# Zero rows at fixed places in the front, x1 split chunk by chunk, and group tables made inside the shared block

## What is computed

```python
xw = gelu(layernorm(ada_emb) @ w1 + b1) @ w2 + b2      # -> x_a, x_b: (b, 512, 8)
layer = base + einsum('bdr,bkr->bdk', x_a, x_b)
x1 = x + (x + einsum('btc,bco->bto', x, layer))

shared = (silu(x1 @ w1) * (x1 @ w3)) @ w2
s = sigmoid(concat([x1, t_emb]) @ router_W)
idx = top_k(s + router_bias, 2)                        # two experts per token
gates = s[idx] / sum(s[idx])
routed = sum over the two experts of gate * (gelu(x1 @ W1e[e]) @ W2e[e])
out = x1 + (shared + routed) / 3
```

## Time and profile before

| what | value |
|---|---|
| median of 3 runs | 1117.33 us (1116.65 to 1117.41) |
| the profiled execution, its own time | 1117.86 us |
| its span in the trace | 1116.1 us |
| TensorE busy with matmuls | 1076.1 us (96% of the span) |
| VectorE, ScalarE, GpSimd busy | 485.5, 398.7, 155.7 us |
| granted TensorE clock, mean | 0.986 of full speed |
| zero rows `xs_d<-zeros` | 8 DMAs of 1024 KB |

### The profile page before, as it was taken

One profiled execution on the slowest core, in us unless ns is written; L12 is line 12 of the kernel. 1 busy time (PEld: TensorE's weight loads), 2 busy tenths in 40 slices (PEclk: granted clock), 3 DMA queues, 4 the chain that ended last, 5 costly groups with the idle time before them and its releaser, 6 DMA issues.

```text
span 1116.1 us, 15418 instructions
## 1 busy us (share of the span) xinstructions
PE 1076.1 (96%) x5226; PEld 879.0 (79%) x5226; DVE 485.5 (44%) x1014; ACT 398.7 (36%) x687; POOL 155.7 (14%) x193
## 2 busy tenths in 40 slices
PE   6999799889799999999999999999999999999998
PEld 5666578778588888888888888888888888888886
DVE  4102654554356645655664533331424333142434
ACT  2211344441366566656666631211212121121211
POOL 3001258370000000000000022011020201102020
PEclk8999899999899999999999999999999999999999
DMA  8663579889768688767657545013050501305041
GB/s 302 267 229 98 186 274 395 300 287 307 208 189 278 191 239 272 223 193 213 212 150 194 183 132 207 1 58 132 0 188 0 187 0 55 133 0 188 0 151 38
DMA packets 131703, 191.42 MB, mean 172 GB/s; under 512 B 9535, under 2 KB 73023, under 8 KB 129879
## 3 DMA queue, kind: packets, MB, share of 16 engines
q1 hardware_dynamic: 120118, 156.38, 43.8%
q0 software_dynamic: 11552, 34.61, 8.3%
HBM read 117.04 MB, written 73.92 MB: 171 GB/s over the span
## 4 chain that ended last, share of the span: by engine, by line
PE 85%; DVE 5%; DMA 3%; SPq 3%; issue 2%; POOL 1%; ACT 1%; DVEq 0%; ACTq 0%; POOLq 0%
PE K L1461 10%; PE K L1462 10%; PE K L1463 10%; PE L L1462 5%; PE L L1463 5%; PE L L1461 5%; PE Rb L1462 5%; PE Rb L1463 5%; PE Rb L1461 5%; PE M L1461 4%; PE M L1463 4%; PE M L1462 4%; PE Rb L1551 3%; PE M L1489 2%; PE M L1491 2%; PE M L1490 2%
## 5 line engine op out<-in xcount | busy, mean ns | idle before, releaser
L462 ACT ACTIVATE slf<-K 128x512 f32<-128x512 f32 x64 | 38.3, 598 | 226.4 <-PE K L1463 221.9
L773 POOL DMA_INDIRECT yb<-ys_d,pos_fix x64 | 61.2, 957 | 322.4 <-DVE total L1392 254.0
L465 ACT CAST gTh<-slf 128x512 fp32r<-128x512 f32 x64 | 39.7, 621 | 184.9 <-DVE slf L475 184.9
L1461 PE MATMUL M<-w2h,gTh 128*128 128x512 f32 x256 | 100.5, 392 | 3.3 <-DVE gTl L477 3.3
L1463 PE MATMUL M<-w2h,gTl 128*128 128x512 f32 x256 | 100.3, 392 | 0.0
L1462 PE MATMUL M<-w2l,gTh 128*128 128x512 f32 x256 | 100.2, 391 | 0.0
L1461 PE MATMUL K<-x1h,w13h 128*128 128x512 f32 x256 | 99.7, 389 | 0.0
L1463 PE MATMUL K<-x1h,w13l 128*128 128x512 f32 x256 | 99.6, 389 | 0.0
L1462 PE MATMUL K<-x1l,w13h 128*128 128x512 f32 x256 | 99.6, 389 | 0.0
L475 DVE TENSOR_TENSOR slf<-L,slf 128x512 f32<-128x512 f32 x32 | 22.1, 692 | 161.8 <-PE L L1463 152.9
L1329 DVE TENSOR_TENSOR e2l<-e2raw,e2h 128x512 fp32r<-128x512 f32 x64 | 41.3, 686 | 79.9 <-ACT e2h L926 79.9
(11 more groups left out here) (244 smaller groups left out, 2470.2 us busy)
## 6 DMA issues: line engine op xcount, KB each, us to landing
w2c<-in_L_cond_w_dram SPq DMA_DIRECT2D x8, 2048.0 KB, 8.6
e1raw<-in_L_cond_W1e_dram SPq DMA_DIRECT2D x16, 1024.0 KB, 7.1
e2raw<-in_L_cond_W2e_dram SPq DMA_DIRECT2D x16, 1024.0 KB, 5.6
xr<-xs_d SPq DMA_DIRECT2D x64, 256.0 KB, 4.4
ys_d<-yo SPq DMA_DIRECT2D x32, 512.0 KB, 7.1
xtok<-in_x_dram SPq DMA_DIRECT2D x32, 256.0 KB, 7.5
x_d<-x1tok SPq DMA_DIRECT2D x8, 1024.0 KB, 8.4
xs_d<-zeros SPq DMA_DIRECT2D x8, 1024.0 KB, 8.8
```

Source lines behind the costliest of these rows:

```text
L462: nc.scalar.activation(slf[:, h % 2], U[h % 2][:], ACT.Silu).then_inc(ffn.silu, 1)
L465: nc.scalar.copy(gTh[:, h % 2], slf[:, h % 2]).then_inc(ffn.g_hi, 1)
L773: pool.indirect_dma_start(out=yb[:, c, :], out_offset=None, in_=ys_d, in_offset=bass.IndirectOffsetOnAxis(ap=pos_fix[:, c:c + 1].bitcast(U ...
L1461: mm(o, ah, bh_, start=start, stop=False)
```

## The change

- The zero rows no longer depend on the counts. SyncE writes the first 512 rows of each of the 8 regions with zeros, in the front: two behind the load of block 2's tokens, six behind the load of block 3's. They come from a zero tile `padz` (128 x 2048) that GpSimd fills at the start and that lies on the memory of `x1tok0`. So ScalarE's first copy into `x1tok0` and GpSimd's first scatter wait for `pad_out`.
- An expert's last group now ends with the expert's last token: where its last group would run past it, the group starts earlier and overlaps the group before. `tables` has more steps for that, and `rows_at_ends` moves the affected rows of `ypos`.
- x1 of block 7 is split chunk by chunk (`cut_last`) inside block 7, behind each `keep_base`, instead of all four chunks behind the block.
- `tables` moves from ahead of the shared block to behind its step 0, together with the cut of piece UP_PIECES + 1. `rows_at_ends` stands behind step 4, `gate_weights` behind step 5.
- SyncE's stream behind block 7: the table's store and load come between the last two `w2` pieces, the zero rows are gone, and `load_rows(0)` comes ahead of `load_e1(0)` and `load_e2(0)`.

```diff
@@ memory
+            with ExitStack() as z:
+                padz = sb("padz", [P, GR // P, D], F32, z)
             x1tok0 = sb("x1tok0", [P, TT, D], F32, st)
...
@@ SyncE, front
             for t in range(TT):
                 load_x(2, t)
+
+            def fill_pads(e):
+                sp.wait_ge(padz_rdy, 1)
+                sp.dma_start(xs_d[e * REGION:e * REGION + GR, :].rearrange("(p r) d -> p r d", p=P), padz[:]
+                             ).then_inc(pad_out, 16)
+            for e in range(2):
+                fill_pads(e)
             for n in range(5, LOADS):
                 load_net(n)
             for t in range(TT):
                 load_x(3, t)
+            for e in range(2, E):
+                fill_pads(e)
...
@@ SyncE, behind block 7
-            for i in range(UP_PIECES + 1, PIECES):
-                load_piece(sp, i)
+            load_piece(sp, UP_PIECES + 1)
             store_tok(NB - 1)
-
+            load_piece(sp, UP_PIECES + 2)
             sp.wait_ge(tabs, 1)
             sp.dma_start(tab_d, tabi[0:TAB]).then_inc(tab_out, 16)
-
-            pad_src = zeros[:].unsqueeze(1).broadcast_to([P, GR * D // (P * P), P])
-
-            def fill_pads(e):
-                alone(sp)
-                row = sp.value_load(padi[0:1, ds(e, 1)], min_val=0, max_val=E * REGION - GR)
-                sp.dma_start(xs_d[ds(row, GR), :].rearrange("(p r) (k c) -> p (r k) c", p=P, c=P), pad_src).then_inc(pad_out, 16)
-            sp.wait_ge(pads, 1)
-            with sp.Fori(0, E // 2) as e:
-                fill_pads(e)
             sp.wait_ge(tab_out, 16)
             sp.dma_start(tab_i[:], tab_d.rearrange("(a p) c -> a (p c)", a=1)).then_inc(tab_in, 16)
-            with sp.Fori(E // 2, E) as e:
-                fill_pads(e)
+            load_piece(sp, UP_PIECES + 3)
...
+            load_rows(0)
             load_e1(0)
             load_e2(0)
-            sp.wait_ge(pad_out, 16 * E)
-            load_rows(0)
...
@@ GpSimd
+            nc.gpsimd.memset(padz[:], 0.0).then_inc(padz_rdy, 1)
             pool.wait_ge(consts, 14)
...
+            pool.wait_ge(pad_out, 16 * E)
             for b in range(NB):
...
@@ ScalarE, keep_tok
                 if t == 0:
-                    if b == 1:
+                    if b == 0:
+                        act.wait_ge(pad_out, 16 * E)
+                    elif b == 1:
...
+            def cut_last(k):
+                act.wait_ge(xp_sb, (NB - 1) * KC + k + 1)
+                act.wait_ge(s_ps, NB)
+                nc.scalar.copy(x1h[:, k], xp[(NB - 1) % EARLY][:, k]).then_inc(x1_hi, 1)
...
                     if h % 2 == 1:
                         keep_base(b, h // 2)
+                        if b == NB - 1:
+                            cut_last(h // 2)
...
-            for k in range(KC):
-                act.wait_ge(xp_sb, (NB - 1) * KC + k + 1)
-                nc.scalar.copy(x1h[:, k], xp[(NB - 1) % EARLY][:, k]).then_inc(x1_hi, 1)
...
@@ tables
-            link(ts(col[ROW], tmp[0], float(E * REGION - GR), None, ALU.min))
+
+            link(ts(top, taken[:], -float(GR), None, ALU.add))
+            link(nc.vector.scalar_tensor_tensor(out=top, in0=iota8[:], scalar=float(REGION), in1=top,
+                                                op0=ALU.mult, op1=ALU.max))
+            link(tt(thr[:, 0:E - 1], top[:, 1:E], top[:, 0:E - 1], ALU.subtract))
+            link(tt(thr[:, 0:E - 1], thr[:, 0:E - 1], past[:, 0:E - 1], ALU.mult))
+            link(red(tmp[1], thr[:, 0:E - 1], AX, ALU.add))
+            link(tt(tmp[1], tmp[1], top[:, 0:1], ALU.add))
+            link(tt(col[ROW], tmp[0], tmp[1], ALU.min))
             link(ts(col[LAST], ends[:, E - 1:E], -1.0, None, ALU.add))
             nc.vector.tensor_copy(tabi[:], tab[:]).then_inc(tabs, 1)
 
-            nc.vector.tensor_scalar(t9, nt, float(GR), -float(REGION), ALU.mult, ALU.add).then_inc(tabs, 1)
+
+            link(ts(off, nt, float(GR), -float(GR), ALU.mult, ALU.add))
+            link(nc.vector.scalar_tensor_tensor(out=thr, in0=iota8[:], scalar=float(REGION), in1=off,
+                                                op0=ALU.mult, op1=ALU.add))
+            link(tt(off, thr, top, ALU.subtract))
+            link(ts(off, off, 0.0, None, ALU.max))
+            link(ts(t9, nt, float(GR), -float(REGION), ALU.mult, ALU.add))
+            tt(t9, t9, off, ALU.subtract).then_inc(tabs, 1)
...
+        def rows_at_ends(dve):
...
+            thr, off = tw[:, 6], tw[:, 7]
+            for e in range(E):
+                link(nc.vector.tensor_scalar(step[:], pos_all[:], thr[:, e:e + 1], off[:, e:e + 1], ALU.is_ge, ALU.mult))
+                link(nc.vector.tensor_tensor(slots[:], slots[:], step[:], ALU.add))
             nc.vector.tensor_copy(ypos[:], slots[:]).then_inc(tabs, 1)
...
@@ VectorE
+            def cut_last(k):
+                dve.wait_ge(x1_hi, k + 1)
+                if k == KC - 2:
+                    corrected(dve, NB - 2)
+                if k == KC - 1:
+                    corrected(dve, NB - 1)
+                tt(x1l[:, k], xp[(NB - 1) % EARLY][:, k], x1h[:, k].bitcast(F32), ALU.subtract).then_inc(x1_lo, 1)
...
+                    if b == NB - 1 and h % 2 == 1:
+                        cut_last(h // 2)
             places(NG - 1)
-            nc.vector.tensor_copy(padi[:], taken[:]).then_inc(pads, 1)
             cut_piece(UP_PIECES)
-            tables(dve)
...
-            after = {h: lambda h=h: cut_piece(UP_PIECES + 1 + h) for h in range(PIECES - UP_PIECES - 1)}
+            def tables_and_cut():
+                tables(dve)
+                cut_piece(UP_PIECES + 1)
+            after = {0: tables_and_cut, 1: lambda: cut_piece(UP_PIECES + 2), 2: lambda: cut_piece(UP_PIECES + 3)}
             after[3] = lambda: rows_in_ys(dve)
-            after[4] = lambda: gate_weights(dve)
+            after[4] = lambda: rows_at_ends(dve)
+            after[5] = lambda: gate_weights(dve)
```

15 lines of the change are left out of this document (9 added, 6 removed).

## The result

| kernel | median of its runs | against the kernel before |
|---|---|---|
| before, beside it | 1116.99 us (1116.65 to 1117.41) | |
| after | 1134.93 us (1130.55 to 1135.64) | 1.015 [1.0128, 1.0171] |

The kernel is 18 us slower; 1112.6 us had been predicted. The profiled execution took 1135.24 us (span 1133.3), 17.4 more than that of before. The losses lie in three stretches, and the gain that was predicted is there as well.

A forecast was written before the change was run, and what follows sets the result against it. TensorE, saturated in the last 800 us, was taken as the bound, so only earlier stretches could gain. 4.78 + 0.3 - 0.3 = 4.8 us off gave 1112.6 us, with 1109.7 to 1115.9 for 8 in 10.

The forecast's parts named there:

- The gap, 4.78 us: TensorE's 8.19 us idle ahead of the first expert group falls to 3.4 us, gaining 4.78 us.
- The clock, 0.3 us: At the first expert group, a shorter gap lets TensorE's clock fall less: 0.3 us gained, bounds 0 to 2.1.
- Three edits and what they move: The prediction's frame: price the change's edits and what they shift; the last 800 us were taken as saturated loops.
- The memset, "nothing": At the start, GpSimd's 1.8 us memset of the zero tile fits inside 7.56 us of its waiting: no cost.
- The zero rows in the front, 0.3 us: Six zero DMAs behind block 3's tokens slow small transfers ahead of the low-rank matmuls: 0.3 us lost, bounds 0 to 3.
- rival 2: The zero rows in the front slow the factors: 2 to 3 us lost, 1115 us; chance 0.12.
- The 2.77 us stall: TensorE's idle time at 240.15 in the shared block, tied to block 5's scatter, stays about 2.8 us.
- x1 split 0: Splitting x1 inside block 7 gives or costs nothing, as the scatter stall absorbs small shifts; without cover about 0.6 us.
- token store 0: Block 7's 1 MB token store, issued at about 233 beside the scatter, costs 0, bounds 2.5 us both ways.
- Table 0: Tables behind step 0 of the shared block leave step 1's low part half a microsecond early: 0 us lost.
- The signs named ahead of the result: Wrong if the first low-rank matmul or shared block starts over 1 us later, or TensorE waits again between 244 and 290.
- Rival 4: ScalarE's first copy into x1tok0 waits for slow zero DMAs and stops the chain of blocks: 1136 us; chance 0.06.

The follow-up runs named there:

- e16: e7 with the split of x1 and the move of the tables also undone; 1110.52 us beside 1116.67 for the kernel before, ratio 0.9957.
- e4: e1 with GpSimd's memset of padz moved behind its b2rep copies; 1119.61 us, 1.0027 of the kernel before.
- e1: The kernel after with 32 bytes per partition put back in padi's place; 1123.68 us, 1.0065 of the kernel before.
- e5: e4 without GpSimd's wait for the zero rows ahead of its first scatter; 1143.59 us beside 1138.57 for the kernel before, ratio 1.0037.
- e7: e5 with the eight zero DMAs also spread in pairs over idle DMA stretches; 1140.13 us beside 1138.57 for the kernel before, ratio 1.0005.
- e14: The same kernel as e5, run again; 1.0025 of the kernel before, which took 1139.20 us beside it.
- e13: The same kernel as e7, run again; 0.9998 of the kernel before, which took 1139.20 us beside it.
- e9: e4 with GpSimd's wait for the zero rows replaced by one for the long-ready constants; 1140.26 us beside 1139.47 for the kernel before, ratio 1.0.
- e2: The kernel before with 32 bytes per partition added behind tab, shifting x1h and all tiles behind; 1130.62 us, 1.0121 of the kernel before.
- e3: e1 with another 32 bytes ahead of all tiles, so weights and inputs both lie at 32 modulo 64; 1121.52 us, 1.0049 of the kernel before.
- e12: e7 with the group tables made ahead of the shared block as before; 0.9982 of the kernel before, which took 1139.47 us beside it.
- e15: The same kernel as e12, run again; 0.9964 of the kernel before, which took 1139.20 us beside it.
- e18: The same kernel as e12, run a third time; 0.9972 of the kernel before, which took 1134.87 us beside it.

## Why the prediction was wrong

- **The gap, 4.78 us: right.** Predicted was an idle time of 3.3 to 3.6 us, ended by the rows' low part, with the turns directly behind the expert weight's low part; it is 3.01 in the kernel after and 3.17 in e16. I had the first matmul of the group at 299.84 us, e16 has 299.18. The rows themselves are asked for at 258.33 in e16 and land well before 275.
- **The clock, 0.3 us: right in size in e16.** There the first group comes 5.4 us earlier and the last stage 5.9, and the first ten matmuls of the group take 3.90 us (before 4.37). It doesn't follow from the gap alone: behind 3.01 us idle the kernel after needs 2.38 us for ten, and behind 3.18 us e4 needs 4.40.
- **"Three edits and what they move" was the frame, and it failed.** The largest loss, 13.2 us in the last stage and 1.2 to 1.4 in the shared block (against e4 and e1, idle time taken out), comes from a line that I did not price at all: `padi` goes, and every tile behind it moves by 32 bytes. I said that the loops "need no more than one row" and held their 443 matmuls fixed. They are a property of the layout, not of the stage. No rival contained it.
- **The memset, "nothing": wrong.** I took GpSimd's 7.56 us of idle time as its cover and looked only at who waits for GpSimd, not at who shares its ports. It holds VectorE for 1.8 us, and the network's result is 1.3 us earlier without it (e4 against e1).
- **The zero rows in the front, 0.3 us (bounds 0 to 3): the term mis-sized.** The factor path lost 2.2 us in the trace of the kernel after and 2.8 in e4's; e5 and e7, e14 and e13 differ by 3.0 to 3.5. The rate of 414 GB/s was about right, as the stretch from 88 to 98 us of the kernel after shows (columns as in the earlier trace rows): 401 GB/s. But the front itself was later, and the last zero rows landed at about 106 us in place of 101.5. What failed was the cost of the small transfers beside them, put at 0.6 us for each of two stores, less 0.7 us of cover. The factor loads wait for the second store, which lands 2.3 us later than before, and 2.2 of these 2.3 reach TensorE, so next to nothing was covered. It was rival 2, to which I gave 0.12.

```profile
88.00:98.00 10.00, 10.00 (x139) 6.52 (x133) 0.00 (x0) 0.58 (x1) 0.00 (x0) 1.00 1.00 401
```

- **GpSimd's wait ahead of its first scatter has no term in the sum**: only ScalarE's wait for the zero rows was weighed. The semaphore was long reached, but the wait is an instruction too. With it and the memset, two instructions more stand ahead of the scatter, and 6.3 us of standstill come there (e9 against e5). Up to 8.1 us of the shared block's delay came from there; that price is argued from the traces, not measured.
- **The 2.77 us stall was to stay.** It did in e16 (2.23). In the kernel after the late start covered it, and with it about 4.5 us of the 12.7 were regained (2.77 idle and 1.7 of slow clock, an estimate).
- **x1 split 0, token store 0:** not contradicted. **Table 0:** borne out by the traces of the kernel after and e4, where TensorE waits nowhere in the shared block; in e1, at step 1, it waits 0.29 us for the low part behind the tables, so the half microsecond of cover was about used up. Two sets on the other chips leave up to 0.3% open.
- **The signs named ahead of the result** did come: I had said that I am wrong if the first low-rank matmul or the shared block starts over a microsecond later. They start at 112.50 and 238.92 us (before 107.93 and 226.21).
- **Rival 4 named the right sign for a wrong reason.** It had 1136 us from ScalarE's wait at `x1tok0`; ScalarE never waited there. That its time is near the measured one is chance.

## What to carry to other kernels

When a tile is added or dropped in a hand-placed layout, compare the addresses of both operands of every matmul before and after; where the count of matmuls in a saturated stretch changes at full clock, look there first. Before a filler operation on GpSimd is called free, look at what VectorE runs beside it, and not only at who waits for GpSimd. When an engine stands still with nothing to wait for, look at the instruction packets in the DMA queues before blaming the semaphore.

## What was not expected of the hardware

- The matmul pace depends on where the operands lie to each other: 443 in 100 us where the two are equal modulo 64 bytes, 430 or 431 where they are 32 apart (e1, e2, e3, and the kernel after).
- A VectorE operation that starts beside a row of GpSimd memsets ended only behind all of them: 4.47 us with one memset of 1.79 us more, 2.79 us without it.
- One instruction more or less ahead of a scatter of GpSimd decides over 6 us of standstill (e4 and e9 against e5). What it costs in all was not measured.
- The same kernel takes 1117 us on some chips and 1135 to 1139 on others, the difference lying in one stretch of 100 us. A gain of 0.43% on the first kind (e16) was 0.18 to 0.36% in the nearest kernels on the second (e12, e15, e18).
